# Second round of a two-layer graph kernel: destination spans of 500 in place of 250, with four larger buffers in the ring in place of eight

## The chip, the cores and the metric

The kernel runs on one core of a Trainium2 chip. The metric is the device time of one execution in microseconds; the kernel before has a median of 1175.72 us over 3 runs (1175.63 to 1184.43).

A core has five engines with queues of their own: PE (TensorE, matrix products), DVE (VectorE), ACT (ScalarE), POOL (GpSimd) and SP (SyncE, which here only issues transfers). They meet through semaphores alone. In the rows below PEld is PE's load of the stationary operand of a product.

## The reference

6250 nodes with 96 features, 106250 edges sorted by destination. Two rounds, each followed by a layer norm:

```python
# round 0
h = gelu(x @ W_pre + b_pre)
aggr = segment_sum(h[src] * edge_attr_96, dst)        # messages with edge features
t = x + aggr
x = layernorm(x + (t + gelu(gelu(t @ W1 + b1) @ W2 + b2)))
# round 1
deg = segment_sum(ones, dst); dinv = rsqrt(max(deg, 1))
h = x @ W_lin.T + b_lin
agg = segment_sum(h[src] * (dinv[src] * dinv[dst])[:, None], dst)
out = layernorm(x + relu(agg + x @ W_root.T + b_root))
```

## The kernel before, in words

**Round 0** goes over the edges in 167 units of 5 tiles of 128 edges. For a unit, POOL issues five indirect transfers (line 880) that gather the rows `h[src]` into `gath`, which has room for 8 units; POOL may fill a unit's place when DVE's product of the unit 8 before is done (`s_msg`). SP loads the edge features into `edg`, ACT copies them to `edges_ps` (L1022), DVE compares the destinations with a window's numbers (`onehot`, L1291) and multiplies (`msg`, L1307), and PE sums `msg` against `onehot` into `seg` (L1517). DVE adds a group's window to `sumT`, the sums by node (L1328). As soon as the nodes of a chunk (4 tiles of 128 nodes; the cuts are in `FINE`) are complete, the "step0" phases compute that chunk's new `x`, the table for round 1 as three bf16 summands `parts`, and the root term.

**Round 1** does not gather again. In the first part of the program, beside round 0, a matrix of counts is built: how many edges go from each source node to each destination. DVE builds one-hot rows (`hots_raw`, L1403, L1405), PE multiplies them for pairs of 5 destinations (`count_pair`, L1549; 625 pairs), ACT turns the result into bf16 (`keep_pair`, L970) in one of two `counts` buffers, and SP stores a buffer of 125 destinations to HBM when it is full (`store_counts`, L739; 50 stores of 1531 KB). The sums of round 1 are then dense products: for a span of destinations and a cut of source tiles, SP loads a **piece** of the counts (`load_piece`, L749), and PE multiplies it with the three summands of `parts` for each tile (`sum_piece`, L1571: stationary operand 96 columns of `parts`, moving operand one row of counts as wide as the span). Pieces of one span that stand behind each other form a run in one PSUM bank; DVE adds a finished run to `sumT` or `upper` (`dense`, L1429, and L1423 where an amount kept apart is taken in). While pairs are still counted, only one bank is there for runs, later three. There are 313 pieces in 170 runs.

**Where the pieces stand** is decided by `schedule()` when the program is built: each unit brings a credit of 11 tiles (14 once all pairs are counted), a piece is put in when the credit is at least `CT` = 4, and one piece may follow each pair. A span is ready four units after its last store. All engines follow the one list `order`; SP issues everything in its order, and the load of piece q waits until piece q - `PS` is used (`s_used`), with `PS` buffers in the ring.

At the end the counts for the last cuts of source tiles are multiplied the other way round (`add_counts`, L1652), and the last layer norm runs set by set ("step1").

Of the kernel before, what the change touches and what calls it, by code (L numbers as in the profile page):

```python
# [6 lines left out]
BF16 = mybir.dt.bfloat16  # L7
# [37 lines left out]
CT = 4  # L45
# [33 lines left out]
DN = 2 * GD  # L79
SPANS = N_NODES // DN  # L80
PS = 8

SPLIT = 12
# [16 lines left out]
EAGER_SPANS = SETS[EAGER] // 2  # L100
# [5 lines left out]
assert NT % CT == 1 and len(TAILS) == 1 and SETS[-1] == STORES and STORES % 2 == 0 and STORES * GD == N_NODES  # L106
# [41 lines left out]

def span_end(e):
    return DN * e + DN  # L150

# [11 lines left out]
def schedule():  # L163
# [67 lines left out]
    for u in range(ALL_UNITS):  # L231
# [69 lines left out]
def build(nc, x, xT_in, src, dst, first, tile_first, tile_rows, edge, edge_tail, W_pre, b_pre, W1, b1, W2, b2,  # L301
          WlinT, b_lin, WrootT, b_root, out):
    with ExitStack() as ctx:
# [27 lines left out]
        piece = piece_raw[:].bitcast(BF16).rearrange("p (s h n) -> p s h n", s=PS, h=2)  # L331
# [240 lines left out]
        def is_apart(k):  # L572

            return apart[k // 2] is not None
# [112 lines left out]
        def _(sp):  # L687
# [118 lines left out]
            for item in order:  # L806
# [10 lines left out]
                while loaded < ahead and 2 * pieces[loaded][0] + 2 <= stores_sent:  # L817
# [401 lines left out]
        def _(dve):  # L1219
# [188 lines left out]
            def dense(r):  # L1408

                e, q, is_apart, takes = runs[r]  # L1410
                run_sum = sums(r)[0:D, 0:DN]
                high = upper[:, (e - SPLIT) * DN:(e - SPLIT) * DN + DN] if e >= SPLIT else None
                if is_apart:
                    total = high
                else:
                    total = sumT[0:D, e * DN:e * DN + DN]
# [41 lines left out]
        def _(pe):  # L1458
# [103 lines left out]
            def sum_piece(q):  # L1562
# [5 lines left out]
                for i in range(tiles_in(c)):  # L1568
                    rows = piece[:, q % PS, :, i * GD:(i + 1) * GD]
                    for part in range(3):  # L1570
                        mm = pe.matmul(sums(r)[0:D, 0:DN], parts[:, FINE[c] + i, part, :], rows,  # L1571
# [69 lines left out]
            def add_counts(c, f):  # L1641
# [5 lines left out]
                for t in reversed(range(tiles)):  # L1647
                    if f < CUTS - 1 and (SETS[c] + t) // 2 >= EAGER_SPANS:
                        continue
# [100 lines left out]
```

## Time and profile before

| | |
|---|---|
| median of the runs | 1175.72 us |
| span of the profiled execution | 1626.2 us |
| PE busy / PEld busy | 1089.4 / 924.8 us |
| POOL busy | 813.4 us |
| DVE busy / ACT busy | 744.1 / 585.3 us |
| moved by DMA | 260.26 MB, mean 160 GB/s |
| mean granted clock of PE | 0.811 |

The profiled execution is 450.5 us longer than the median run, so busy shares of its span say little about an execution that isn't profiled. What can be read from it are durations of single instructions, distances between instructions that follow each other with nothing between, and the order in which engines wait for each other.

### The profile page before, as it was taken

To read this page: it belongs to the slowest core of one execution; us is meant where nothing else is said; L and a number is where in the kernel's file an instruction comes from. 1 tells how busy PE (TensorE), PEld (TensorE's weight loads), DVE (VectorE), ACT (ScalarE), POOL (GpSimd) and SP (SyncE) were. 2 spreads that over 40 slices of the span, in tenths; PEclk is the share of its full clock that TensorE was granted. 3 is DMA by queue.
4 is the path that set the end of the run, shared out by engine and by line. 5 is a ranking of instruction groups with operands and counts; after the bars stand their busy time and mean duration, and the time that the engine had idled before them with its cause. 6 is when DMAs were issued, how large, how long until landed. Compare 5 with 4: busy or idle time off the path is not lost. (4 is left out here: it accounts for less than half of the span.)

```text
span 1626.2 us, 21159 instructions
## 1 busy us (share of the span) xinstructions
PE 1089.4 (67%) x7455; PEld 924.8 (57%) x8121; DVE 744.1 (46%) x1460; ACT 585.3 (36%) x1012; POOL 813.4 (50%) x908
## 2 busy tenths in 40 slices
PE   3341465655656766677767777877877876747887
PEld 3341343433444644566657666767777776646787
DVE  6024555546645646455535444532323324233466
ACT  0130355655646556365534445541001011010124
POOL 7355356556555646545534534545555444565202
PEclk9985666777776887878978988988889888878899
DMA  5421165545445547557656556756666655544553
GB/s 151 124 77 29 37 200 169 182 138 187 149 142 182 180 136 230 179 162 239 208 165 200 163 186 212 219 174 189 192 179 187 167 160 147 158 114 128 133 153 77
DMA packets 185721, 260.26 MB, mean 160 GB/s; under 512 B 68650, under 2 KB 163882, under 8 KB 179018
## 3 DMA queue, kind: packets, MB, share of 16 engines
q1 hardware_dynamic: 158328, 215.57, 41.9%
q0 software_dynamic: 26992, 42.82, 11.4%
q8 instruction: 63, 1.03, 0.3%
q10 hardware_dynamic: 290, 0.45, 0.1%
q14 instruction: 48, 0.39, 0.1%
HBM read 173.12 MB, written 85.62 MB: 159 GB/s over the span
## 5 line engine op out<-in xcount | busy, mean ns | idle before, releaser
L880 POOL DMA_INDIRECT gath<-table_h,srcs x791 | 757.2, 957 | 712.2 <-DVE msg L1307 491.4
L1571 PE MATMUL bank_q<-piece_raw,early_late 128*96 128x250 bf16 x3453 | 460.2, 286 | 74.4 <-issue 55.6
L1571 PEld LDWEIGHTS bank_q<-piece_raw,early_late 128*96 128x96 bf16 x3453 | 403.0, 131 | 76.8 <-issue 72.8
L1517 PE MATMUL seg<-onehot,msg 128*97 128x128 f32 (+1 forms) x1662 | 297.5, 341 | 136.9 <-DVE sumT L1328 63.7
L970 ACT CAST counts_raw<-bank_q 128x490 bf16<-128x490 f32 x400 | 281.1, 747 | 268.7 <-PE bank_q L1549 117.6
L1307 DVE TENSOR_TENSOR msg<-gath,edges_ps 128x480 f32<-128x480 f32 x166 | 107.8, 650 | 411.3 <-ACT edges_ps L1022 351.0
L1517 PEld LDWEIGHTS seg<-onehot,msg 128*97 128x97 f32 x1662 | 258.0, 215 | 60.6 <-DVE msg L1307 32.9
L1549 PE MATMUL bank_q<-hots_raw 128*128 128x245 bf16 x834 | 183.5, 319 | 141.5 <-ACT counts_raw L970 101.1
L970 ACT CAST counts_raw<-bank_b 128x490 bf16<-128x490 f32 x200 | 149.8, 749 | 144.0 <-remote 49.8
L1022 ACT COPY edges_ps<-edg 128x480 f32<-128x480 f32 x166 | 98.8, 595 | 262.7 <-DVE msg L1307 227.2
L1405 DVE TENSOR_TENSOR hots_raw<-counters,kb 128x1960 bf16<-128x1960 bf16 (+1 forms) x157 | 182.6, 1163 | 0.0
L1549 PEld LDWEIGHTS bank_q<-hots_raw 128*128 128x128 bf16 x834 | 72.4, 107 | 192.9 <-ACT counts_raw L970 137.3
L1464 PEld LDWEIGHTS <-w_pre 97*128 97x128 bf16 x666 | 69.4, 112 | 162.4 <-DVE sumT L1328 66.7
L1549 PE MATMUL bank_b<-hots_raw 128*128 128x245 bf16 x416 | 95.8, 318 | 88.2 <-ACT counts_raw L970 53.9
L1429 DVE TENSOR_TENSOR sumT<-sumT,bank_q 96x250 f32<-96x250 f32 x126 | 51.7, 411 | 190.5 <-remote 114.1
L1291 DVE TENSOR_TENSOR onehot<-counters,rel 128x640 f32<-128x640 f32 (+1 forms) x166 | 131.6, 793 | 0.0
L1403 DVE TENSOR_TENSOR hots_raw<-counters,kb 128x1024 bf16<-128x1024 bf16 (+1 forms) x157 | 106.8, 680 | 52.8 <-remote 35.5
L1549 PEld LDWEIGHTS bank_b<-hots_raw 128*128 128x128 bf16 x416 | 35.6, 107 | 115.0 <-ACT counts_raw L970 72.1
L1328 DVE TENSOR_TENSOR sumT<-sumT,seg 97x128 f32 (+1 forms) x62 | 17.1, 275 | 73.8 <-remote 59.7
L1429 DVE TENSOR_TENSOR upper<-upper,bank_q 96x250 f32<-96x250 f32 x31 | 12.7, 410 | 73.5 <-remote 50.5
L859 POOL DMA_INDIRECT gath<-in_x,srcs x40 | 38.5, 963 | 12.9 <-issue 11.9
L892 POOL TENSOR_TENSOR gap<-bns 125x5 f32<-125x5 f32 x9 | 1.8, 201 | 74.2 <-DVE bns L1189 74.2
(212 smaller groups left out, 655.6 us busy)
## 6 DMA issues: line engine op xcount, KB each, us to landing
counts_hbm<-counts_raw SPq DMA_DIRECT2D x50, 1531.2 KB
piece_raw<-counts_hbm SPq DMA_DIRECT2D x250, 250.0 KB
edg<-in_edge SPq DMA_DIRECT2D x166, 240.0 KB
gath<-table_h,srcs POOLq DMA_INDIRECT x791
piece_raw<-counts_hbm SPq DMA_DIRECT2D x38, 125.0 KB
piece_raw<-counts_hbm SPq DMA_DIRECT2D x25, 187.5 KB
counts_raw<-counts_hbm SPq DMA_DIRECT2D x4, 625.0 KB
table_h<-stage SPq DMA_DIRECT2D x12, 192.0 KB
```

The lines of the kernel that those rows point to most:

```text
L880: pool.indirect_dma_start(gath[0:k, u % GS * UT + j, :], None, table[0], bass.IndirectOffsetOnAxis(ap=srcs[0:k, t:t + 1], axis=0)).then_in ...
L970: act.copy(counts[:, k % 2, :, i * WD:(i + 2) * WD].rearrange("p a (w n) -> p w a n", w=2), counted).then_inc(s_kept, 1)
L1022: act.copy(edges_ps[:, 0:UT * D], edg[:, u % ES].rearrange("p j d -> p (j d)")).then_inc(s_eps, 1)
L1291: dve.tensor_tensor(onehot[:, s, :, 0:w], iota_ps[:, 0:w].unsqueeze(1).to_broadcast([P, UT, w]), rel[:, u * UT:(u + 1) * UT].unsqueeze(2). ...
L1307: dve.tensor_tensor(msg[:, s, :, 0:D], gath[:, slot_tiles(u), :], by_tile(edges_ps, UT), ALU.mult).then_inc(s_msg, 1)
L1403: dve.tensor_tensor(hot_b(j)[:, 0:n], iota_b.unsqueeze(1).to_broadcast([P, n, P, 2]), blocks.unsqueeze(2).to_broadcast([P, n, P, 2]), ALU. ...
L1405: dve.tensor_tensor(hot_k(j)[:, 0:n], iota_k.unsqueeze(1).to_broadcast([P, n, KC, 2]), keys.unsqueeze(2).to_broadcast([P, n, KC, 2]), ALU. ...
L1429: dve.tensor_tensor(total, total, run_sum, ALU.add).then_inc(s_dense, 1)
L1464: pe.ldweights(w_pre[:].bitcast(BF16)[:, 0:P])
L1517: last = pe.matmul(seg[0:D + 1, half(g)], msg[0:k, u % MS, j, :], onehot[0:k, u % MS, j, 0:reach(g)], start=(u == first_unit(g) and j == 0 ...
L1549: last = pe.matmul(pair_bank(m)[:, w * KC:(w + 1) * KC], hot_b(j)[:, i, :, w], hot_k(j)[:, i, :, w], start=True, stop=True)
L1571: mm = pe.matmul(sums(r)[0:D, 0:DN], parts[:, FINE[c] + i, part, :], rows, start=(first and i == 0 and part == 0), stop=(last and i == til ...
```

## The change

A span is now four stores wide: 500 destinations, in 13 spans, of which the last has two stores (250). A piece of four tiles has 500 KB, and the ring has four of them in place of eight of 250 KB, the same memory. The schedule counts a piece of a full span with twice its tiles, and asks for a credit of 8.

```diff
-DN = 2 * GD
-SPANS = N_NODES // DN
-PS = 8
-SPLIT = 12
+HALVES = 4
+DN = HALVES * GD
+SPANS = -(-STORES // HALVES)
+PS = 4
+SPLIT = 6
...
+def span_sets(e):
+    return range(HALVES * e, min(HALVES * e + HALVES, STORES))
...
+def span_nodes(e):
+    return slice(DN * e, span_end(e))
+def cost_of(e, c):
+    return tiles_of_cut(c) * len(span_sets(e)) // 2
...
-            if ready and stored[2 * e + 1] + 4 <= u:
-                gain = FINE[upto(e)] - FINE[summed[e]]
+            if ready and stored[span_sets(e)[-1]] + 4 <= u:
+                gain = (FINE[upto(e)] - FINE[summed[e]]) * len(span_sets(e)) // 2
...
-            if credit >= CT:
+            if credit >= 2 * CT:
...
-                    credit -= tiles_of_cut(pieces[-1][1])
+                    credit -= cost_of(*pieces[-1][0:2])
                 else:
-                    credit = min(credit, 2.0 * CT)
+                    credit = min(credit, 4.0 * CT)
...
-                    sp.wait_ge(s_store[s], 16 * (e + 1))
+                    sp.wait_ge(s_store[s], 16 * len(range(s, span_sets(e).stop, 2)))
...
-                sp.dma_start(piece[:, q % PS, :, 0:tiles_in(c) * GD],
-                             counts_hbm[2 * e:2 * e + 2, :, cols].rearrange("h b n -> b h n")
+                sp.dma_start(piece[:, q % PS, 0:len(sets), 0:tiles_in(c) * GD],
+                             counts_hbm[sets.start:sets.stop, :, cols].rearrange("h b n -> b h n")
...
-                        mm = pe.matmul(sums(r)[0:D, 0:DN], parts[:, FINE[c] + i, part, :], rows,
+                        mm = pe.matmul(sums(r)[0:D, 0:len(span_sets(e)) * GD], parts[:, FINE[c] + i, part, :], rows,
```

The list that results has 163 pieces in 92 runs. Of its 1797 products 1656 are 500 wide and 141 are 250 wide; before there were 3453, all 250 wide. The columns are the same: 2 x 1656 + 141 = 3453 widths of 250. Destinations whose sum is kept apart for a while (`upper`) are the same ones, as are the products of the end.

On PE, in a unit of the stage in which pairs are still counted (before, unit 100). `hots_raw` products are pairs, `piece_raw` products are pieces, `seg` is round 0's unit:

```order
L1517 MATMUL seg<-onehot,msg 97x128 x5
L1464 LDWEIGHTS w_pre
L1549 MATMUL bank_b<-hots_raw 128x245 x2
L1464 LDWEIGHTS w_pre
L1571 MATMUL bank_q2<-piece_raw,early_late 96x250 x9
L1549 MATMUL bank_q0<-hots_raw 128x245 x2
L1571 MATMUL bank_q2<-piece_raw,early_late 96x250 x12
L1549 MATMUL bank_q1<-hots_raw 128x245 x2
L1571 MATMUL bank_q2<-piece_raw,early_late 96x250 x12
L1549 MATMUL bank_b<-hots_raw 128x245 x2
L1571 MATMUL bank_q2<-piece_raw,early_late 96x250 x12
```

The same place after the change:

```order
L1532 MATMUL seg<-onehot,msg 97x128 x5
L1479 LDWEIGHTS w_pre
L1564 MATMUL bank_b<-hots_raw 128x245 x2
L1586 MATMUL bank_q2<-piece_raw,early_late 96x500 x12
L1564 MATMUL bank_q0<-hots_raw 128x245 x2
L1586 MATMUL bank_q2<-piece_raw,early_late 96x500 x12
L1564 MATMUL bank_q1<-hots_raw 128x245 x2
L1564 MATMUL bank_b<-hots_raw 128x245 x2
L1479 LDWEIGHTS w_pre
L1564 MATMUL bank_q0<-hots_raw 128x245 x2
L1564 MATMUL bank_q1<-hots_raw 128x245 x2
```

Between two pairs there now stand twelve products of 500 columns where twelve of 250 stood, and fewer places hold a piece.

On PE behind the last pair (before, units 127 and 128), three runs are touched in two units:

```order
L1517 MATMUL seg<-onehot,msg 97x128 x5
L1571 MATMUL bank_q1<-piece_raw,early_late 96x250 x12
L1464 LDWEIGHTS w_pre
L1571 MATMUL bank_q2<-piece_raw,early_late 96x250 x24
L1464 LDWEIGHTS w_pre
L1571 MATMUL bank_q0<-piece_raw,early_late 96x250 x12
L1464 LDWEIGHTS w_pre
L1517 MATMUL seg<-onehot,msg 97x128 x5
L1571 MATMUL bank_q0<-piece_raw,early_late 96x250 x12
```

After the change, the same units:

```order
L1532 MATMUL seg<-onehot,msg 97x128 x5
L1479 LDWEIGHTS w_pre
L1586 MATMUL bank_q0<-piece_raw,early_late 96x500 x24
L1479 LDWEIGHTS w_pre
L1532 MATMUL seg<-onehot,msg 97x128 x5
L1479 LDWEIGHTS w_pre
L1586 MATMUL bank_q1<-piece_raw,early_late 96x500 x12
```

Here a unit holds one or two pieces where it held three or four, and each `LDWEIGHTS w_pre` ahead of a run, which waits for the bank, is there half as often.

## Rows read from the trace of the kernel before

**Rows 1.** The page's costliest groups: busy us, mean ns | idle before, releaser

```profile
L880 POOL DMA_INDIRECT gath<-table_h,srcs x791 | 757.2, 957 | 712.2 <-DVE msg L1307 491.4
L1571 PE MATMUL bank_q<-piece_raw,early_late 128*96 128x250 bf16 x3453 | 460.2, 286 | 74.4 <-issue 55.6
```

**Rows 2.** POOL in order of time, its first gathers: start, us, [idle before <-releaser]

```profile
94.82 0.95 POOL L880 DMA_INDIRECT gath<-table_h,srcs  x1 [35.05 <-DVE msg L1307]
96.07 0.95 POOL L880 DMA_INDIRECT gath<-table_h,srcs  x1 [0.30 <-issue]
...
137.36 0.94 POOL L880 DMA_INDIRECT gath<-table_h,srcs  x1 [0.30 <-issue]
146.22 5.63 POOL L880 DMA_INDIRECT gath<-table_h,srcs  x1 [7.92 <-DVE msg L1307]
...
178.46 0.94 POOL L880 DMA_INDIRECT gath<-table_h,srcs  x1 [20.62 <-DVE msg L1307]
```

**Rows 3.** POOL in order of time, its last gather

```profile
1528.07 1.11 POOL L880 DMA_INDIRECT gath<-table_h,srcs  x1 [9.95 <-DVE msg L1307]
```

**Rows 4.** The chain that ended last: the last unit, the first and last products of the end

```profile
1577.40 0.14 DVE onehot L1298
...
1580.12 0.23 DVE sumT L1328
1580.35 0.12 issue
1580.47 1.45 PE bank_q L1632 x10
...
1612.14 1.74 PE bank_q L1652 x30
```

**Rows 5.** Timeline at 1300 us: pieces on PE in a stretch at full pace, and one where they stop

```profile
1300.09 2.56 PEld L1571 LDWEIGHTS bank_q<-piece_raw,early_late 128*96 128x96 bf16 x24
1303.95 0.52 PE L1571 MATMUL bank_q<-piece_raw,early_late 128*96 128x250 bf16 x3 [0.43 <-issue]
1305.38 0.59 PE L1571 MATMUL bank_q<-piece_raw,early_late 128*96 128x250 bf16 x4 [0.91 <-issue]
1307.50 0.78 PE L1571 MATMUL bank_q<-piece_raw,early_late 128*96 128x250 bf16 x4 [1.53 <-issue]
...
1317.92 1.12 PEld L1517 LDWEIGHTS seg<-onehot,msg 128*97 128x97 f32 x10
1319.10 5.60 PE L1571 MATMUL bank_q<-piece_raw,early_late 128*96 128x250 bf16 x48
...
1322.73 0.64 DVE L1307 TENSOR_TENSOR msg<-gath,edges_ps 128x480 f32<-128x480 f32 x1
1325.17 0.68 DVE L1108 TENSOR_TENSOR colsT<-sumT,xTc 97x512 f32<-97x512 f32 x1
1326.50 0.64 DVE L1307 TENSOR_TENSOR msg<-gath,edges_ps 128x480 f32<-128x480 f32 x1
```

**Rows 6.** Timeline at 949 us: pieces between pairs

```profile
949.27 0.20 PEld L1549 LDWEIGHTS bank_q<-hots_raw 128*128 128x128 bf16 x2
949.49 1.31 PEld L1571 LDWEIGHTS bank_q<-piece_raw,early_late 128*96 128x96 bf16 x12
950.47 0.61 ACT L1022 COPY edges_ps<-edg 128x480 f32<-128x480 f32 x1
950.78 0.20 PEld L1549 LDWEIGHTS bank_q<-hots_raw 128*128 128x128 bf16 x2
951.00 1.31 PEld L1571 LDWEIGHTS bank_q<-piece_raw,early_late 128*96 128x96 bf16 x12
951.12 0.66 DVE L1307 TENSOR_TENSOR msg<-gath,edges_ps 128x480 f32<-128x480 f32 x1 [0.62 <-issue]
```

**Rows 7.** Line views of L970 and L1429: duration ns min/median/max

```profile
L970 ACT CAST counts_raw<-bank_q x400: 697/736/853, 184.1 to 1094.0; 128x490 bf16<-128x490 f32 x134
L1429 DVE TENSOR_TENSOR sumT<-sumT,bank_q x126: 404/411/415, 554.0 to 1578.7; 96x250 f32<-96x250 f32 x126
```

**Rows 8.** Transfers by line: KB each, us from issue to landing

```profile
edg<-counts_hbm SPq DMA_DIRECT2D x1, 312.5 KB, 5.4
edg<-counts_hbm SPq DMA_DIRECT2D x1, 187.5 KB, 5.0
```

**Rows 9.** Stretches: us, PE (x) PEld (x) DVE (x) ACT (x) POOL (x), PEclk, DMA share, GB/s

```profile
700.00:800.00 100.00, 78.23 (x519) 65.05 (x560) 57.95 (x97) 56.35 (x96) 56.52 (x60) 0.83 0.67 212
1100.00:1200.00 100.00, 81.56 (x599) 73.07 (x625) 28.52 (x66) 9.21 (x17) 54.35 (x58) 0.87 0.65 190
```

More of the change, by code:

```diff
@@ L99 @@
 EAGER = 5
-EAGER_SPANS = SETS[EAGER] // 2
+EAGER_SPANS = SETS[EAGER] // HALVES
 LOADED = (0, 1, 2, 3, 7, 4, 5, 6)
@@ L105 @@
 assert REM > 0 and UT * D <= 512 and EARLY <= GS and NW * WD == N_NODES
-assert NT % CT == 1 and len(TAILS) == 1 and SETS[-1] == STORES and STORES % 2 == 0 and STORES * GD == N_NODES
+assert NT % CT == 1 and len(TAILS) == 1 and SETS[-1] == STORES and STORES * GD == N_NODES
 assert CUTS - 1 == next(c for c in range(CUTS) if FINE[c] == NT - 2) and FINE[CUTS - 2] == NT - 4
@@ L146, in last_pair_of @@
     return (k * GW + GW - 1) // 2
+def span_sets(e):
+    return range(HALVES * e, min(HALVES * e + HALVES, STORES))
 def span_end(e):
-    return DN * e + DN
+    return GD * span_sets(e).stop
+def span_nodes(e):
+    return slice(DN * e, span_end(e))
+def cost_of(e, c):
+    return tiles_of_cut(c) * len(span_sets(e)) // 2
 def span_chunk(e):
@@ L330, in build @@
         piece_raw = sb("piece_raw", [P, PS * CT * DN // 2])
-        piece = piece_raw[:].bitcast(BF16).rearrange("p (s h n) -> p s h n", s=PS, h=2)
+        piece = piece_raw[:].bitcast(BF16).rearrange("p (s h n) -> p s h n", s=PS, h=HALVES)
         hots_raw = sb("hots_raw", [P, 2 * BP * (P + KC)])
@@ L572, in is_apart @@
         def is_apart(k):
-            return apart[k // 2] is not None
+            return apart[k // HALVES] is not None
         def tiles_in(c, cuts=FINE):
@@ L748, in load_piece @@
                 cols = slice(FINE[c] * GD, FINE[c + 1] * GD)
-                sp.dma_start(piece[:, q % PS, :, 0:tiles_in(c) * GD],
-                             counts_hbm[2 * e:2 * e + 2, :, cols].rearrange("h b n -> b h n")
+                sets = span_sets(e)
+                sp.dma_start(piece[:, q % PS, 0:len(sets), 0:tiles_in(c) * GD],
+                             counts_hbm[sets.start:sets.stop, :, cols].rearrange("h b n -> b h n")
                              ).then_inc(s_piece[q % PS], 16)
@@ L816, in _ @@
                     ahead = min(item[1] + PS, len(pieces))
-                while loaded < ahead and 2 * pieces[loaded][0] + 2 <= stores_sent:
+                while loaded < ahead and span_sets(pieces[loaded][0]).stop <= stores_sent:
                     load_piece(loaded)
@@ L1410, in dense @@
                 e, q, is_apart, takes = runs[r]
-                run_sum = sums(r)[0:D, 0:DN]
-                high = upper[:, (e - SPLIT) * DN:(e - SPLIT) * DN + DN] if e >= SPLIT else None
+                nodes = span_nodes(e)
+                run_sum = sums(r)[0:D, 0:nodes.stop - nodes.start]
+                high = upper[:, nodes.start - SPLIT * DN:nodes.stop - SPLIT * DN] if e >= SPLIT else None
                 if is_apart:
@@ L1415, in dense @@
                 else:
-                    total = sumT[0:D, e * DN:e * DN + DN]
+                    total = sumT[0:D, nodes]
                     dve.wait_ge(s_base, span_chunk(e) + 1)
@@ L1568, in sum_piece @@
                 for i in range(tiles_in(c)):
-                    rows = piece[:, q % PS, :, i * GD:(i + 1) * GD]
+                    rows = piece[:, q % PS, 0:len(span_sets(e)), i * GD:(i + 1) * GD]
                     for part in range(3):
-                        mm = pe.matmul(sums(r)[0:D, 0:DN], parts[:, FINE[c] + i, part, :], rows,
+                        mm = pe.matmul(sums(r)[0:D, 0:len(span_sets(e)) * GD], parts[:, FINE[c] + i, part, :], rows,
                                        start=(first and i == 0 and part == 0),
@@ L1647, in add_counts @@
                 for t in reversed(range(tiles)):
-                    if f < CUTS - 1 and (SETS[c] + t) // 2 >= EAGER_SPANS:
+                    if f < CUTS - 1 and (SETS[c] + t) // HALVES >= EAGER_SPANS:
                         continue
```

## The prediction

> **What bounds the kernel now.** I read the page's costliest groups first, because the profiled span (1626.2 us) is 450.5 us longer than the median run, and busy shares of such a span mislead. The largest group is POOL's gathers: 791 of them, 0.957 us each, and most of their idle time is a wait for DVE's product [rows 1]. So either POOL sets the pace, or whoever frees its buffers does.
>
> Next POOL in order of time. Gathers that wait for nothing follow each other at a strict distance: from 94.82 to 137.36 us there are 35, so 42.54 / 34 = 1.251 us each, 0.95 busy and 0.30 between [rows 2]. Five make 6.26 us a unit. Then POOL has filled its 8 places and waits for DVE, which is held up by the preparation of the count tables; the gathers run on from 178.46 us [rows 2]. By then 40 of 791 are issued, and 751 are left. If POOL never waited again it would need 751 x 1.251 = 939.5 us, up to 1118.0. In the profile the last gather starts at 1528.07, and waits for DVE even there [rows 3]: POOL had been a full 8 units ahead, and the others set the pace of the profiled execution.
>
> From the last unit's work (1577.40) to the end of the span there are 48.8 us of chain, all of it DVE and PE one behind the other [rows 4]. Put behind a POOL that never waits: 1118.0 + 1.1 for the last gather + about 3 for its landing and the product (my estimate: half of the 5.0 us of the smaller transfer in [rows 8], and 0.6 for the product) + 48.8 = 1171 us. The median is 1175.72. In other terms: of the profile's excess, 1349.6 - 939.5 = 410 us are POOL's waits and 46 us the eight units still open at the end, together 456 of the 450.5 by which the two executions differ. **The execution that is timed looks like one in which the gathers set the pace from 178 us on**, with some 5 us left for everything else. I can't see it directly; it rests on a head and a pace that I take over unchanged from the profile.
>
> Can the others keep 6.26 us a unit? PE makes 24 weight loads of pieces in 2.56 us, 0.107 us a product, and 48 products in 5.60 us [rows 5]. At the stage of units 80 to 109 the list holds 972 products, 32.4 a unit: 3.5 us. Add 1.1 to 1.2 for the unit's own ten loads [rows 5], 6.15 pairs at 0.22 (1.4 us) [rows 6], and some 0.2 for waits and the chunk's steps: 6.2 to 6.4 us. In units 110 to 139, with 1230 products, it is 4.4 + 1.2 + 0.3 = 5.9. So PE is about as loaded as POOL and has eight units of room to be late in, 50 us. Singly, units do reach such paces in the profile: two products of DVE stand 3.77 us apart at 1322.73 and 1326.50 [rows 5]. But pieces also stop with nothing to wait for, three or four products and then 0.4 to 1.5 us of "issue" [rows 5]; I take these stops as belonging to the profiled execution, since the median has no room for them.
>
> **The change, part by part.**
>
> *Wider products.* 250 columns take 0.107 us, of which 250 / 2.4 GHz = 0.104 are columns; the granted clock is 0.83 to 0.87 in the mean of these stages [rows 9], and these rows are at its upper level. So weight loads are already hidden and only 0.003 us a product is left to win. 500 columns: 0.208 + 0.003 = 0.211 at best, 2 x 0.107 = 0.214 at worst. PE's sum goes from 3453 x 0.107 = 369.5 to 1656 x 0.211 + 141 x 0.107 = 364.5 us: 5 us less, bounds 0 and 5. That the weight side is not the limit shows at the other end too: the 96-column products of the end take 1.74 / 30 = 0.058 us [rows 4], far below 0.107, so loading is quick enough for 250 columns.
>
> The Trainium skill, "TensorE: Matmul & The Clock Gate", Back-to-back issue gap, gives a stream of load and product pairs as about 131 ns each at 512 columns and 81 ns at 128. By that the 1656 wide products would take 217 us and PE would gain some 137; the row at 250 columns (0.107) is what its columns alone take and doesn't lie on a line between those two, so I don't count on it.
>
> *Runs.* 92 in place of 170: 78 waiting weight loads fewer, 0.04 us each, 3 us of PE. DVE adds 92 sums in place of 170. At 250 columns one takes 0.411 us [rows 7]; a 512-column sum from SBUF takes 0.68 [rows 5], which I take for 500. 170 x 0.411 = 69.9 becomes 92 x 0.68 = 62.6: 7 us less on an engine that is under 60% busy [rows 9]. Worth nothing while POOL sets the pace.
>
> *Transfers.* The same bytes in 163 issues in place of 313. SP's issues are not on the path. A piece of 500 KB lands later: 187.5 KB take 5.0 us and 312.5 KB 5.4 [rows 8], so 0.4 per 125 KB, and 500 KB about 6.0. When PE begins piece q, piece q + 3 may be loaded; three pieces of 12 x 0.211 make 7.6 us of cover, and behind the last pair, where a unit has two pieces, there are the units' own products besides. Before it was 7 x 1.28 = 9.0 us of cover for about 5.2. The cover shrinks from 3.8 to 1.6 us and still holds; if it failed by 1 us a piece in the 56 pieces of units 110 to 139, that is 56 us, little more than the eight units of room.
>
> *The order.* Between two pairs there are now 2.53 us of piece in place of 1.28. ACT copies the next unit's edge features behind the second pair, so the way from one unit's product on PE to the next unit's is: 1.2 (unit) + 0.22 + 2.53 + 0.22 + 0.74 (ACT's pair) + 0.61 + 0.66 (DVE's product) [rows 5 to 7] = 6.2 us, with handovers 6.4. Before it was 1.25 less, 5.1. Units with two or three pieces (11 of the 32 units 80 to 111) take PE 1.2 + 1.4 + 2 x 2.53 + 0.2 = 7.9 us. Mean: (21 x 6.4 + 11 x 7.9) / 32 = 6.9, that is 0.65 over POOL's pace and 21 us over the stage. This lateness fits into the 50 us of room, and behind unit 112 PE needs 5.9 us a unit and catches up 0.36 x 35 = 13 us by unit 146; units 147 to 150 hold no piece and give the rest back.
>
> Sum on the path that sets the end: 0 from PE and DVE, 0 from the transfers, 0 from the order while the room lasts, 0 from the end, which is the same. 1175.72 + 0 = **1175 us**.
>
> **The rivals.**
>
> *POOL doesn't set the pace, its users do* (faster). If the head is shorter in the timed execution than in the profile, the 5 us left over grow, and PE, at 6.2 to 6.4 us a unit in units 80 to 109, is the bound there. Then PE's 8 us (5 + 3) count, and the 48 products that leave this stage (972 become 924 widths) move 5 us into units with room: 1175 - 13 = 1162 us. For it: PE is the busiest engine of the profile in both stages [rows 9]. Against it: the sum of the gathers hits the median within 5 us. Chance 0.20 for a gain over 1%.
>
> *A wide product is cheaper than its columns* (faster still), as the page has it: on a POOL-bound kernel it gives nothing, on a PE-bound one down to the gathers' 1171 less what the head hides, so about 1160. Chance 0.03, within the 0.20.
>
> *Thicker pieces starve ACT and DVE while pairs are counted* (slower). The mechanism is the 2.53 us between two pairs, as above. It decides when the consumers enter unit 80 with less than 21 us of room, that is when the first stage has not let them catch up with POOL. Then all of it shows: 1175 + 21 = 1196 us; with half of the room gone, 1187. For it: POOL starts this stage a full eight units ahead at 178.46 us [rows 2], so the consumers start with no room at all. Against it: the stage to unit 80 has no or few pieces. Chance 0.17. *A ring of four that runs dry* behind unit 112 would cost up to 56 us, less what the room takes: 1180 to 1200. Chance 0.05.
>
> *The change does nothing*: that is my forecast, chance 0.58.
>
> **How the numbers follow.** About 1% is what a measurement of this kernel can tell from no change, so the borders are 1164 and 1187. Likeliest 1175 (0.58, own range 1168 to 1182). Faster 0.20, slower 0.22. For 8 in 10 the range takes the gain of PE with the moved products and a little more (1160), and the full price of the thicker pieces (1198).
>
> **What would show it.** In the changed kernel's profile: 500-wide products at 0.211 to 0.214 us in unbroken stretches (0.13 would be the page's rule); gathers still 1.25 us apart where they don't wait; DVE's sums at about 0.68 us. The profiled span may well fall by tens of us, since PE's stops come between its instructions and there are 1656 products and 1734 weight loads fewer; that would say nothing of the median. Thicker pieces show as longer waits of ACT's L970 and of DVE's product for `edges_ps` between 600 and 1100 us, a dry ring as PE idle ahead of L1586 with a landing as its end. Wrong would be the forecast if the timed execution were not paced by the gathers, above all if their 0.30 us gaps were shorter without the profiler.

## The result, and the profile after

The changed kernel takes **1217.84 us** (median of 4 runs, 1214.60 to 1221.01), against 1177.18 for the kernel before in the runs it is compared with. The ratio is 1.035 with a 95% interval of 1.030 to 1.040: about 41 us slower. The prediction said 1175 us, no change.

The profiled execution of before whose rows stand above was a disturbed one (its span of 1626.2 us is far from any timed run), so the kernel before was profiled again; from here on "before" is this second profile, with a span of 1180.4 us, and the 32.4 us between it and the profile of after (1212.8 us) are what has to be explained. (The medians differ by 41 us; the second profile is an execution from the slower end of before's runs, that of after its fastest.)

The pages' costliest groups, busy us and mean ns, then idle before and its main releaser. Before, second profile, where [rows 1] had 460.2 us of products and 712.2 us of idle POOL:

```profile
L880 POOL DMA_INDIRECT gath<-table_h,srcs x791 | 760.2, 961 | 284.8 <-issue 231.3
L1571 PE MATMUL bank_q<-piece_raw,early_late 128*96 128x250 bf16 x3453 | 409.1, 273 | 9.1 <-DVE early_late L1163 3.7
```

After:

```profile
L894 POOL DMA_INDIRECT gath<-table_h,srcs x791 | 758.6, 959 | 308.9 <-issue 228.0
L1586 PE MATMUL bank_q<-piece_raw,early_late 128*96 128x500 bf16 (+1 forms) x1797 | 400.6, 375 | 6.5 <-DMA piece_raw<-counts_hbm 3.5
L1444 DVE TENSOR_TENSOR sumT<-sumT,bank_q 96x500 f32<-96x500 f32 x65 | 43.6, 670 | 95.5 <-PE bank_q L1586 94.8
```

The stops inside pieces of [rows 5] are gone from both: they belonged to the disturbed execution, as supposed. PE's pieces wait for nothing worth naming. So the loss isn't in the time of the products, and hardly in the ring: PE waits 3.5 us for landings.

**Where the time went.** The borders of the windows are the products (`msg`) of units 80, 110, 150 and the last one, then the end; columns as in [rows 9]. Before:

```profile
571.00:797.00 226.00, 199.88 (x1679) 180.36 (x1793) 145.48 (x240) 145.64 (x237) 143.82 (x152) 0.98 0.83 261
797.00:1030.00 233.00, 227.49 (x2049) 222.67 (x2192) 113.20 (x265) 42.12 (x71) 173.49 (x183) 1.00 0.89 261
1030.00:1132.00 102.00, 88.63 (x734) 84.75 (x830) 62.29 (x183) 20.28 (x36) 56.74 (x60) 0.92 0.68 178
1132.00:1180.00 48.00, 37.66 (x529) 37.00 (x573) 29.04 (x139) 22.30 (x65) 11.55 (x63) 0.92 0.36 88
```

After, the same four stretches:

```profile
570.00:821.00 251.00, 207.90 (x1176) 136.74 (x1283) 146.76 (x234) 141.49 (x236) 142.18 (x151) 0.94 0.74 233
821.00:1051.00 230.00, 226.83 (x1346) 159.71 (x1450) 106.99 (x223) 41.75 (x70) 172.16 (x181) 1.00 0.87 263
1051.00:1161.00 110.00, 92.06 (x491) 63.25 (x558) 58.88 (x154) 20.28 (x36) 57.91 (x61) 0.88 0.63 169
1161.00:1213.00 52.00, 41.07 (x516) 40.30 (x561) 27.65 (x135) 22.30 (x65) 11.56 (x63) 0.86 0.32 78
```

Unit 80 starts 1.5 us earlier than before. Then come 25 us of loss in units 80 to 109 (8.36 us a unit where it was 7.53), 3 us of gain in units 110 to 149, 8 us of loss from unit 150 to the last product (unit 166), and 4 in the end. In the first stretch PE is idle for 43 us in place of 26, and no other engine is fuller: nobody is busy, everybody waits. For whom, the waits say (us in total, times, longest). Before:

```profile
DVE msg L1307 <- ACT edges_ps L1022: 213.0, 76, 31.6
ACT counts_raw L970 <- PE bank_q L1549: 133.7, 115, 5.2
POOL gath L880 <- DVE msg L1307: 53.4, 32, 5.5
```

After:

```profile
DVE msg L1321 <- ACT edges_ps L1036: 247.0, 81, 31.6
ACT counts_raw L984 <- PE bank_q L1564: 160.1, 92, 4.5
POOL gath L894 <- DVE msg L1321: 80.9, 43, 5.5
```

All three waits grow by 26 to 34 us, and they are links of one chain: DVE's product waits for ACT's copy of the edge features, ACT for PE's pair, POOL for DVE. The timeline of one turn in after shows the links (start, us, engine, line; in brackets idle time and who ended it):

```profile
760.90 0.65 DVE L1321 TENSOR_TENSOR msg<-gath,edges_ps 128x480 f32<-128x480 f32 x1 [3.87 <-ACT edges_ps L1036]
...
761.47 0.66 DVE L1444 TENSOR_TENSOR sumT<-sumT,bank_q 96x500 f32<-96x500 f32 x1
...
762.06 0.68 DVE L1417 TENSOR_TENSOR hots_raw<-counters,kb 128x1024 bf16<-128x1024 bf16 x1
762.66 1.17 DVE L1419 TENSOR_TENSOR hots_raw<-counters,kb 128x1960 bf16<-128x1960 bf16 x1
...
763.92 0.40 PE L1564 MATMUL bank_q<-hots_raw 128*128 128x245 bf16 x2 [0.54 <-DVE hots_raw L1419]
...
764.16 2.07 PE L1586 MATMUL bank_q<-piece_raw,early_late 128*96 128x500 bf16 x9
...
766.07 0.38 PE L1564 MATMUL bank_b<-hots_raw 128*128 128x245 bf16 x2
...
766.49 0.73 ACT L984 CAST counts_raw<-bank_b 128x490 bf16<-128x490 f32 x1 [1.40 <-PE bank_b L1564]
...
767.07 0.61 ACT L1036 COPY edges_ps<-edg 128x480 f32<-128x480 f32 x1
767.71 0.65 DVE L1321 TENSOR_TENSOR msg<-gath,edges_ps 128x480 f32<-128x480 f32 x1 [1.47 <-ACT edges_ps L1036]
```

**The loop.** DVE's product, the sum of a finished run, `hots_raw` in two steps, first pair, a whole piece, second pair, ACT's cast of it, ACT's copy into `edges_ps`, DVE's next product. From start to start: 0.57 + 0.59 + 0.60 + 1.26 + 0.24 + 1.91 + 0.42 + 0.58 + 0.64 = 6.81 us. The piece here has nine products; with twelve it is 0.64 more, 7.4 us. With a piece of 1.28 us in place of 2.53, as in before, the same sum gives 6.2 (worked out, not read from a turn of before). Measured are 8.36 and 7.53 us a unit; the 0.9 to 1.3 us between are not split further. Candidates are steps of the chunks that lie in some units' way (DVE's and PE's of L1159 and L1491, for example) and, in after, pieces that run at the lower clock (its mean is 0.94 in this stretch, that of before 0.98). Of all links ACT's copy is the odd one: it needs nothing of the pairs and stands behind the second of them only because `schedule()` puts it at place 2 of each unit.

### The profile page after: what moved, and what is told of

It reads as the page before. It is cut to its first block and busy times, and to the rows that moved or that the text cites. A ratio compares the mean times of both kernels' runs of the same rounds, so it can differ in the third digit from the quotient of the medians.

```text
span 1212.8 us, 17246 instructions
## 1 busy us (share of the span) xinstructions
PE 979.9 (81%) x5799; PEld 699.8 (58%) x6387; DVE 732.7 (60%) x1376; ACT 578.2 (48%) x1012; POOL 814.6 (67%) x908
## 5 line engine op out<-in xcount | busy, mean ns | idle before, releaser
L1586 PE MATMUL bank_q<-piece_raw,early_late 128*96 128x500 bf16 (+1 forms) x1797 | 400.6, 375 | 6.5 <-DMA piece_raw<-counts_hbm 3.5
L1532 PE MATMUL seg<-onehot,msg 128*97 128x128 f32 (+1 forms) x1662 | 252.8, 308 | 81.8 <-DVE msg L1321 46.4
L1586 PEld LDWEIGHTS bank_q<-piece_raw,early_late 128*96 128x96 bf16 x1797 | 218.6, 125 | 139.3 <-issue 13.2
L1532 PEld LDWEIGHTS seg<-onehot,msg 128*97 128x97 f32 x1662 | 223.3, 190 | 47.6 <-DVE msg L1321 46.0
L1564 PE MATMUL bank_q<-hots_raw 128*128 128x245 bf16 x834 | 168.2, 299 | 62.1 <-ACT counts_raw L984 50.4
L1564 PEld LDWEIGHTS bank_q<-hots_raw 128*128 128x128 bf16 x834 | 68.8, 104 | 121.1 <-ACT counts_raw L984 97.3
L1564 PE MATMUL bank_b<-hots_raw 128*128 128x245 bf16 x416 | 89.6, 300 | 29.4 <-ACT counts_raw L984 24.6
L1479 PEld LDWEIGHTS <-w_pre 97*128 97x128 bf16 x588 | 58.0, 107 | 95.2 <-DVE sumT L1342 34.0
L1444 DVE TENSOR_TENSOR sumT<-sumT,bank_q 96x500 f32<-96x500 f32 x65 | 43.6, 670 | 95.5 <-PE bank_q L1586 94.8
L996 ACT ACTIVATE y<-bank_a,b1c 96x512 f32<-96x512 f32 (+2 forms) x14 | 8.8, 630 | 38.5 <-PE bank_a L1601 38.5
```

Source lines behind the costliest of these rows:

```text
L1444: dve.tensor_tensor(total, total, run_sum, ALU.add).then_inc(s_dense, 1)
L1479: pe.ldweights(w_pre[:].bitcast(BF16)[:, 0:P])
L1532: last = pe.matmul(seg[0:D + 1, half(g)], msg[0:k, u % MS, j, :], onehot[0:k, u % MS, j, 0:reach(g)], start=(u == first_unit(g) and j == 0 ...
L1564: last = pe.matmul(pair_bank(m)[:, w * KC:(w + 1) * KC], hot_b(j)[:, i, :, w], hot_k(j)[:, i, :, w], start=True, stop=True)
L1586: mm = pe.matmul(sums(r)[0:D, 0:len(span_sets(e)) * GD], parts[:, FINE[c] + i, part, :], rows, start=(first and i == 0 and part == 0), sto ...
```

## The experiments

**0. Before once more**, unchanged, for the second profile.

> The kernel before, unchanged, for a second profile, since the first one's span is 450 us over its median. All theories: a time of 1174 to 1185 us and, if the first profile was disturbed, a span close to that. Theory A (thick pieces between two pairs starve ACT): units 80 to 110 take 6.3 to 7.3 us each here against 8.2 to 8.7 in the changed kernel, and ACT waits for PE's pairs less there. Theory B (the ring of four): the same units, but the difference is PE's idle time ahead of its pieces. Theory C (wide spans become ready later, with one bank for runs): the difference is waits for a run's bank and for DVE's sums.

Measured: 1182.22 us in that one execution, span 1180.4; its rows are those of before shown above.

The theory: **the loop through ACT's copy paces units 80 to 109; its length grows with the PE time of a piece between two pairs, whatever the width of a product.** Rivals: the wide products or spans themselves cost the time; the ring of four is too small for 500 KB; the two stages only trade a fixed amount of PE work. Pieces can be made thick and thin at either width, so the two can be told apart. "Pace" below is the time from the product of unit 80 to that of unit 110, divided by 30, from each run's profile.

**1. After, pieces in halves between pairs.** A piece of four tiles is loaded as before, but PE does two of its tiles at one place and the other two at the next, with a pair between:

```diff
-            if credit >= 2 * CT:
+            if owed:
+                rest()
+            elif credit >= 2 * CT:
...
-                for i in range(tiles_in(c)):
+                half = (tiles_in(c) + 1) // 2
...
+                for i in (range(half) if part_of_it == 0 else range(half, tiles_in(c))):
```

> The changed kernel, but a piece is multiplied in two halves of at most two tiles with one pair between them while pairs are counted; spans, ring, transfers, widths and runs are those of the changed kernel. Theory A (2.5 us of piece between two pairs leave ACT without work, and the next unit's edge copy late): 1175 to 1192 us. Theories B (ring of four) and C (spans of 500 and their runs): 1205 to 1225 us, as the changed kernel.

Measured: 1180.78 us, ratio to before 1.001 (0.998 to 1.005). Pace 7.34 us, below the 7.53 of before. Wide products, the ring of four and 500 KB are all still in, and the loss is gone. That already speaks against width and ring as its cause in this stage: units 80 to 109 take 220 us in place of 251. Units 150 to the end still take 159 us, against 162 in after and 150 in before.

**2. Before, made thick.** Two 250-wide pieces of one place, with a credit of 8, so 2.56 us of PE between two pairs:

```diff
-            if credit >= CT:
+            if credit >= 2 * CT:
...
+                    if len(pieces) > was and (open_run or u > built + 1):
+                        next_piece(u, next(n for until, n in LEAST if u < until))
...
-                    credit -= tiles_of_cut(pieces[-1][1])
+                    credit -= sum(tiles_of_cut(x[1]) for x in pieces[was:])
```

> The kernel before with its spans of 250 and its ring of eight, but the schedule waits for a credit of 8 and then puts two pieces behind each other at one place, so that 2.57 us of piece stand between two pairs as in the changed kernel. Theory A: 1198 to 1220 us. Theories B, C and D (the 500-wide product itself, its clock or its DVE sum): 1172 to 1183 us, as the kernel before.

Measured: 1210.01 us, ratio 1.025 (1.020 to 1.030), pace 8.3 us. The loss appears without any wide product: of the 33 us between the profiles, 24 lie in units 80 to 109, as in after. It is experiment 1 the other way round. Units 150 to 166 are slower too, 111.6 us where before took 101.6; see "The late loss".

**3. Before with a ring of four.** `PS = 4` in place of 8, still 250 KB each, memory layout unchanged.

> The kernel before with a ring of four buffers of 250 KB in place of eight, half the memory ahead that both kernels have. Theory A: 1174 to 1186 us. Theory B (too little ahead): at least 20 us slower, 1196 to 1230 us.

Measured: 1221.43 us, ratio 1.040 (1.032 to 1.048), pace 7.8 us. Here PE does wait for the loads:

```profile
L1571 PE MATMUL bank_q<-piece_raw,early_late 128*96 128x250 bf16 x3453 | 415.2, 274 | 38.5 <-DMA piece_raw<-counts_hbm 29.9
```

So a ring can cost as much as the whole result, and a view that the ring doesn't matter on this kernel is wrong. But these are four pieces of half the size: 3 x 1.28 = 3.8 us of cover against the 5.0 to 5.4 of [rows 8]. In after the same wait is 3.5 us (page row above), since its cover is 3 x 2.53 us.

**4. After in halves, ring of three.** Experiment 1's order (in its general form, as in experiment 5) with `PS = 3`.

> The changed kernel with split pieces (1180.78 with a ring of four) and a ring of three buffers of 500 KB. Theory B in its weak form (the ring of four is at its edge): 1195 to 1230 us, with waits of PE for landings. If four buffers of 500 KB have cover to spare, as forecast (7.6 us against 6.0): 1179 to 1190 us.

Measured: 1196.81 us, ratio 1.015 (1.009 to 1.020), 16 us behind experiment 1; PE's wait for landings is now 14.4 us in 10 places. With two pieces of cover (2 x 2.53 = 5.1 us) the ring is too small. That three are enough isn't shown by this run, whose time lies in the range expected for a ring of four at its edge, but by after itself, where PE waits 3.5 us for landings in all. The prediction's sum on the ring holds.

**5. The same halves everywhere.** In experiment 1 pieces are whole again once all pairs are counted. Here they stay in halves to the end.

```diff
-            if not pairs:
-                rest()
```

> The changed kernel with pieces in halves through the whole program: behind the last pair too the second half stands one place later, so that the steps of a chunk in the last units come between halves (1.27 us) and not whole pieces (2.53 us). The split while pairs are counted alone gave 1180.78, with a last stage from unit 150 of 111 us against 102 in the kernel before. If the thick pieces among the steps cause that: 1165 to 1176 us. If it is the sum of work in the last units: 1177 to 1185 us.

Measured: 1181.72 us, ratio 1.003 (0.999 to 1.007): the same as experiment 1. Nothing is to be had from halves where no pairs are counted. The late loss isn't removed by halving the pieces: units 150 to the end take 162 us, as in after.

**6 to 9. The dose.** Thinner still: after in single tiles (0.64 us) while pairs are counted, then everywhere; and before in halves, which is also 0.64 us. `PART` is the number of tiles done at one place:

```diff
+PART = 1
...
-                for i in range(tiles_in(c)):
+                for i in range(k * PART, min(k * PART + PART, tiles_in(c))):
```

> The changed kernel with pieces in single tiles (0.63 us each, 500 wide) between pairs while pairs are counted, whole behind them. The same thickness as in the split kernel before, with wide products. Theory A with the dose from 2.53 us (1217.84) over 1.27 us (1180.78): 1160 to 1176 us. If 500-wide spans cost something of their own while pairs are counted (readiness, one bank), it stays 5 us or more above the split kernel before.

> The changed kernel with pieces in single tiles of 0.63 us everywhere, one at a place, so that they also stand between the steps of the last units. With single tiles while pairs are counted only it gave 1170.77; its units 150 to 166 and the end took 109 + 52 us where the split kernel before took 99 + 48, with one wait of PE of 3.75 us and a lower clock behind it. If few thick pieces leave nothing to put between the steps of the last units: 1156 to 1166 us, and the 3.75 us wait is gone. If it is something else of the wide spans: 1168 to 1175 us.

> The kernel before (spans of 250, ring of eight) with its pieces in halves of at most two tiles, 0.64 us of piece between two pairs in place of 1.28. Theory A (time of piece between two pairs, against 0.74 us of ACT a pair): ACT is never without a pair, units 80 to 110 fall from 7.5 us towards 7.0, so 1160 to 1172 us. If thickness matters only beyond 1.3 us, or if something else limits ACT: 1174 to 1182 us, as the kernel before.

Measured: 1170.77 us (0.993, 0.990 to 0.996), 1167.93 us (0.991, 0.987 to 0.996), and for before in halves 1154.76 us (0.978, 0.971 to 0.985), below the 1160 to 1172 expected for it. **And before in single tiles** (0.32 us between pairs):

> The kernel before with single tiles of 250 columns (0.32 us) between pairs. Dose of theory A: 1.28 us gave 1178, 0.64 us gave 1154.76. ACT needs 0.74 us a pair, PE 0.22; with 0.32 us of piece a pair PE is ahead of ACT and blocked by the three banks until the parts owed run out. No more gain is expected: 1150 to 1160 us, and over 1160 if single tiles run out of places between the pairs.

Measured: 1140.98 us, ratio 0.970 (0.961 to 0.979), below the 1150 to 1160 expected. The paces, each from one profile, make one table:

| between two pairs | with 500 wide | with 250 wide |
|---|---|---|
| 2.5 us | 8.36 (after) | 8.3 (experiment 2) |
| 1.3 us | 7.34 (experiment 1) | 7.53 (before) |
| 0.64 us | 6.97 (single tiles) | 6.9 (halves) |
| 0.32 us | | 6.45 (single tiles, with less work) |

The last row can't be read as a dose. A narrow piece in four single tiles takes four places, and the list then has room for fewer pieces: in units 80 to 109 PE makes 738 products of 250 columns where before in halves makes 918, which alone is 180 x 0.107 = 19 us, 0.6 us a unit and so more than the 0.45 between the paces. The pieces moved into later units (629 behind unit 150 in place of 517). In the other runs of the table the stage holds 900 to 984 widths of 250.

In the rows above it, the columns agree within 0.2 us at each thickness, and from 2.5 to 0.64 us of PE between pairs the pace falls by 1.4 us for 1.9. The pace goes by thickness, not by width. The totals don't agree as well: at 0.64 us, after is 16 us behind before (18.5 in the profiles), of which these 30 units hold only 2. 7 us lie ahead of unit 80, 4 are won back in units 110 to 149, and 14 lie behind unit 150. See "The late loss".

**10. After with the copy first.** The link itself: ACT's copy for the next unit stands ahead of the unit's first pair in place of behind the second. Nothing else changes; pieces are whole and wide.

```diff
-            if i == 2 and 0 < u < UNITS:
+            if i == 0 and 0 < u < UNITS:
                 order.append(("edges", u + 1))
```

> The changed kernel with whole thick pieces; only the place of ACT's copy of the next unit's edge features moves ahead of the unit's first pair, from behind the second. It tells apart two ways in which thick pieces hurt. If the loss is that the copy, and with it DVE's product and the gathers' buffers, wait behind a pair that stands behind 2.53 us of piece: 1185 to 1200 us. If it is that ACT has no pair to turn in those 2.53 us and so can't turn all pairs of a unit in time: 1210 to 1222 us.

Measured: 1144.09 us, ratio 0.973 (0.964 to 0.981), and so 74 us less than after by one number in the list, far below the 1185 to 1200 us expected even if the copy's place was the cause. DVE's and POOL's waits of before and after shrink or vanish; the page's row and two waits:

```profile
L894 POOL DMA_INDIRECT gath<-table_h,srcs x791 | 762.4, 964 | 243.0 <-issue 238.4
```

```profile
DVE msg L1321 <- ACT edges_ps L1036: 75.1, 32, 31.5
ACT counts_raw L984 <- PE bank_q L1564: 109.5, 69, 3.8
```

POOL's idle time is 243.0 us, of which 238.4 are the 0.30 us steps between gathers: it hardly waits for anyone any more. And the timeline shows the copy and the product beside the piece, not behind it:

```profile
704.23 0.62 ACT L1036 COPY edges_ps<-edg 128x480 f32<-128x480 f32 x1
...
705.04 2.07 PE L1586 MATMUL bank_q<-piece_raw,early_late 128*96 128x500 bf16 x9
...
705.24 0.73 ACT L984 CAST counts_raw<-bank_q 128x490 bf16<-128x490 f32 x1 [0.40 <-PE bank_q L1564]
...
706.96 0.38 PE L1564 MATMUL bank_b<-hots_raw 128*128 128x245 bf16 x2
707.05 0.64 DVE L1321 TENSOR_TENSOR msg<-gath,edges_ps 128x480 f32<-128x480 f32 x1
```

Where the gain lies says why it is larger than the loss that was looked for. Of the 71 us between the profiles of after and of this run, 38 lie in units 80 to 109 and 32.5 ahead of unit 80, a stretch in which after loses nothing against before: units 50 to 79 take 6.43 us each here, 6.96 in before and 7.08 in after. So the copy's place costs time in both kernels and over a longer stretch; thick pieces only lengthen its loop further from unit 80 on.

ACT's cast of the pairs still waits 109.5 us for PE. So the form of the theory in which thick pieces starve ACT, the words of the prediction's slower rival, falls for the most part: ACT still waits that long in a kernel that is 74 us faster, because the copy doesn't stand behind the wait.

**11 and 12. The same edit in before, and its opposite.**

> The kernel before with the edge copy ahead of the first pair, nothing else. Theory L (the loop through DVE's tables, the first pair, a piece, the second pair and the edge copy paces units 50 to 110 in both kernels): 1125 to 1145 us. If wide spans cost something of their own, this stays below the changed kernel with the copy first (1144.09) by 5 us or more; if they don't, the two are equal within 5 us. If the loop paces only the changed kernel: 1170 to 1180 us.

> The kernel before with the edge copy one place later, behind the third pair: its loop gets another piece of 1.28 us, a pair of 0.22 and 0.74 us of ACT in units that hold three pieces or more, and 0.74 to 1 us in the others. Theory L: 1 to 2 us a unit in units 80 to 110 and some in 50 to 80, so 1205 to 1240 us. If the loop does not pace the kernel before: 1174 to 1182 us.

```diff
-            if i == 2 and 0 < u < UNITS:
+            if i == 3 and 0 < u < UNITS:
```

Copy first in before: 1135.04 us, ratio 0.965 (0.958 to 0.972). Copy behind the third pair, so that two pieces of 1.28 us lie in the loop: 1218.77 us, ratio 1.035 (1.026 to 1.045), pace 8.1 us. The same units, about 80 to 110, in the first and in the second:

```profile
536.00:745.00 209.00, 191.36 (x1656) 174.13 (x1770) 144.72 (x240) 143.09 (x235) 158.41 (x167) 1.00 0.88 281
```

```profile
594.00:837.00 243.00, 204.81 (x1694) 185.90 (x1810) 144.95 (x240) 146.47 (x237) 142.10 (x151) 0.96 0.78 246
```

Units 80 to 109 take 209 us in the first and 243 in the second, against 226 in before. So the loop through the copy is lengthened and shortened by the copy's place alone, in an otherwise unchanged kernel. That the second ends at the time of after (1217.84 us) is a coincidence of totals: it loses 23 us ahead of unit 80 and 17 in units 80 to 109 (0.56 us a unit, less than the 1 to 2 expected) and nothing behind them, where after loses nothing ahead of unit 80, 25 in that stage and 12 behind unit 150.

Experiments 10 and 11 together give what the thick, wide pieces cost in units 80 to 109 without the loop: 212.9 us against 208.9. Of the 25 us of loss in this stage, 21 are gone when the copy goes first. With experiments 1 and 2, I take the loop as shown for this stage.

**13 to 15. Both edits together.**

> The kernel before with pieces in halves (1154.76) and the edge copy ahead of the first pair. If the copy's place costs something at this thickness: 1140 to 1152 us. If ACT's pairs alone limit: 1152 to 1158 us.

> The changed kernel with the edge copy first and its pieces in single tiles of 0.63 us everywhere, so that they also fill places between the steps of the last units. Against the changed kernel with the copy first alone (1144.09): if thick and few pieces among the last steps cost what the traces suggest (8 to 10 us and a lower clock), 1130 to 1140 us; else 1141 to 1147 us.

> The kernel before with single tiles between pairs and the edge copy first. With halves and the copy first it gave 1126.28, with single tiles alone 1140.98. The gathers alone give about 62 + 791 x 1.25 + 52 = 1103 us. 1115 to 1128 us.

Before in halves with the copy first: **1126.28 us, ratio 0.957 (0.948 to 0.965)**, the fastest kernel here, 4.3% under the one before. Before in single tiles with the copy first: 1131.49 us (0.962, 0.954 to 0.969). After in single tiles with the copy first: 1133.27 us (0.965, 0.957 to 0.973). All three are within 7 us. The first beat the 1140 to 1152 us expected, the second missed its 1115 to 1128. In the last one the chain of the page leads back to the gathers; its shares of the span by engine:

```profile
POOL 41%; PE 25%; issue 14%; DVE 6%; DMA 4%; ACT 3%; DVEq 0%; SPq 0%; ACTq 0%
```

The last gather starts at 1063 to 1064 us in each kernel with the copy first, whatever its width, and at 1103.83 in before and 1126.30 in after:

```profile
1064.29 0.90 POOL L894 DMA_INDIRECT gath<-table_h,srcs  x1 [0.30 <-issue]
```

(this is experiment 10's). From the first gather at 61.9 that is 1002.4 / 790 = 1.269 us each. POOL waits for nobody there; most steps are 1.25 us, and a few longer ones, up to 5.5 us, raise the mean. These kernels have reached the gathers' pace.

**The late loss.** 12 us of the 32 lie behind unit 150, and they stay when the loop is cut: with the copy first and whole pieces, after is 9 us slower than before (1144.09 against 1135.04). In the last units PE of after has a gap that before has not, and runs slowly behind it:

```profile
1141.58 1.90 PE L1532 MATMUL seg<-onehot,msg 128*97 128x64 f32 x10 [3.75 <-DVE sumT L1342]
```

The same unit in before:

```profile
1114.27 0.85 PE L1571 MATMUL bank_q<-piece_raw,early_late 128*96 128x250 bf16 x6 [1.79 <-DVE sumT L1429]
1115.52 1.07 PE L1517 MATMUL seg<-onehot,msg 128*97 128x64 f32 x10 [0.40 <-DVE sumT L1328]
```

Ten products of a unit take 1.90 us in place of 1.07. The granted clock (behind the five engines) in after from 1141 and in before from 1114:

```profile
1141.00:1147.00 6.00, 4.50 (x18) 3.56 (x20) 3.41 (x11) 0.94 (x2) 0.00 (x0) 0.50 0.39 101
```

```profile
1114.00:1119.00 5.00, 3.22 (x25) 2.67 (x30) 3.56 (x11) 1.01 (x3) 0.00 (x0) 1.00 0.56 143
```

0.50 is the 1.2 GHz level, 1.00 the one of 2.4 GHz. Neither the width of a product nor the ring of four is needed for this. The trace of experiment 2, with 250-wide spans, eight buffers and a credit of 8, has the same gap and the same clock behind it, and its units 150 to 166 take 111.6 us, where after takes 109.6 and before 101.6:

```profile
1141.94 1.87 PE L1519 MATMUL seg<-onehot,msg 128*97 128x64 f32 x10 [3.74 <-DVE sumT L1330]
```

```profile
1142.00:1148.00 6.00, 4.57 (x18) 3.42 (x19) 3.43 (x12) 0.68 (x2) 0.00 (x0) 0.50 0.32 80
```

What experiment 2 shares with after, and before does not, is that the list asks for a credit of 8 and puts eight tiles' worth of piece in at one time, half as often. The gap of 3.74 or 3.75 us is there too in experiments 1, 4, 5, 6 and 10, which keep that credit; with single tiles everywhere (7 and 14) it is 3.1 us. So the late loss in units 150 to 166 goes with the coarser list, not with wide spans; the likely way, that PE has no piece left to lay between the short phases of the last chunks, is argued and no run tests it. Thin pieces hardly touch it: units 150 to the end take 163 us in experiment 7 and 158 in 14, against 162 in after. Of the 12.7 us between the profiles of experiments 10 and 14, 13 lie ahead of unit 110 (with 2 lost and 2 won behind it), so the range that 14 hit was hit for another reason than the one expected.

The 4 us of the end are a matter of the clock. In the first 8 to 10 us behind the last unit's product the granted clock is 0.66 in after and 0.57 in experiment 2, and their ends take 52.0 and 52.7 us; it is 1.00 in before and in experiments 1 and 10, and the ends take 48.5, 48.0 and 48.1. But it is also 0.72 in experiment 13, which is narrow, and the end takes 53.2 us. So these 4 us don't belong to the width either, and not for certain to the change.

## Why the prediction was wrong, point by point

**What bounds the kernel: wrong, by a coincidence.** The prediction took the head from a disturbed profile: a first gather at 94.82 and free running from 178.46 us [rows 2]. In the undisturbed profile of before the first one comes at 61.99:

```profile
61.99 0.94 POOL L880 DMA_INDIRECT gath<-table_h,srcs  x1 [2.28 <-DVE msg L1307]
```

The distance of 1.251 us was right for most steps. With the true head the gathers alone give 62.0 + 790 x 1.251 = 1050.3 for the last one, and 1103 with the 52.9 us that the sum put behind it, not 1171. The last gather of before in fact starts at 1103.8 and 76.6 us follow it. So 53.5 + 23.7 = 77 us that the sum lacked stood against a head that was 68 us too long (1118.0 against 1050.3), and the sum met the median within 5 us by luck. Experiment 11, in which POOL waits for nobody, splits the 77: its last gather starts at 1063.6 and 69.2 us follow. 13 us are the few longer steps between gathers, 40 are POOL's waits for the loop, 16 are missing behind the last gather even without the loop, since the last product comes 21 us after it and not 4, and 7 are the loop's there. The prediction said itself that head and pace weren't seen in a timed execution; it should have asked for more than one total to agree.

**"The order": the right mechanism, and this step of it mis-sized.** "The way from one unit's product on PE to the next unit's is: ... = 6.2 us, with handovers 6.4. Before it was 1.25 less, 5.1." The way closes not on PE's unit product but on DVE's tables: behind its product DVE still has a run's sum (0.67) and `hots_raw` (0.68 + 1.17) to do before the next unit's first pair can start. These 2.45 us (0.59 + 0.60 + 1.26 in the timeline) were left out and PE's 1.2 us, which lie beside them, put in. So the 6.2 should have read 7.4 and the 5.0 without handovers 6.2, and with the steps that hang in the loop they measure 8.36 and 7.53. At 5.1 the loop lay below POOL's 6.26 and was no bound of before; measured at 7.53 it was the bound already, and experiment 11 shows it by taking 42 us from before with the copy's place alone.

**"0 from the order while the room lasts", "This lateness fits into the 50 us of room": wrong, and this is the step that cost the forecast.** The lateness was put at 21 us, and the stage gave 25. That is near, but in part by luck: it was 0.65 us a unit over POOL's 6.26, where the runs have 0.83 over the loop's own 7.53. The room was not there. POOL's lead in before is used up by unit 90: DVE's product starts 43 to 44 us behind the end of its unit's last gather at unit 80 in both kernels, 52 (before) and 61 (after) at unit 90, and 53 and 62 at unit 110, where the eight places are full. With the copy first it is 9 us at unit 80 in both. The prediction named the condition, "when the consumers enter unit 80 with less than 21 us of room", and gave it 0.17. With the loop at its right length it would have seen that the room is eaten before unit 80.

**Wide products: right.** 23 in a row take 5.06 us in after, with 0.37 for the last one (5.06 - 0.37) / 22 = 0.213 us each; predicted were 0.211 to 0.214.

```profile
875.21 5.06 PE L1586 MATMUL bank_q<-piece_raw,early_late 128*96 128x500 bf16 x23
```

The Trainium skill, "TensorE: Matmul & The Clock Gate", Back-to-back issue gap, gives 131 ns for a stream of load and product pairs at 512 columns, and about N / 2.4 + 2.5 ns for a single one. The measured stream follows the second form (an estimate of 211 ns at 500 by that page), not the first.

**Runs and DVE's sums: the price right.** 0.670 us each against 0.68 predicted. "Worth nothing" isn't shown: such a sum stands in the loop, though the columns of the table differ by 0.2 us at most. **The ring: right**, experiments 3 and 4 bracket it. **PE's gain where it is bound**: units 110 to 149 gave 3 us.

**The end: "0 from the end, which is the same": the products are the same, and the profiles of after and before differ by 4 us there,** with the clock as said above. The 8 us of units 150 to 166 are a cost of the coarser list for which the prediction has no term.

The range ended at 1198 with the whole price of the rival. It would have needed the rival's price, the late loss, and a median of before that isn't tied to the gathers.

## What to carry to other kernels

A loop between engines has to be followed until it returns to the instruction it began with, with everything that each engine does in order in between, for both kernels; if the loop of before then comes out below its measured pace, a link is missing. Where work is put between two small steps that others wait for, its longest undivided piece counts: here, changing the size from 2.5 us to 1.3 was worth 37 us, and moving one 0.6 us copy of another engine ahead of the wait 74 us. A total alone doesn't tell causes apart: two kernels that end at 1218 and 1219 us lost their time in different stages. And a sum that meets a measured total proves little when its inputs come from an execution 450 us longer: profile again before building on it.

## What the runs showed of the hardware that was not expected

- A profiled execution can be disturbed as a whole: two profiles of one unchanged kernel had spans of 1626.2 and 1180.4 us, first gathers at 94.82 and 61.99 us, and 460.2 and 409.1 us for the same 3453 products. The distances of instructions that wait for nothing (1.25 us for gathers, 0.107 to 0.108 us for products) were the same in both.
- A gap of 3.75 us on PE was followed by a stretch at the 1.2 GHz level in which a unit's ten products took 1.90 us in place of 1.07. The same gap was followed by a granted clock of 0.50 in experiment 2 (from 1142 to 1148 us) and in experiment 10 (from 1075 to 1085 us). In the first two the products of the same unit took 1.90 and 1.87 us, so there the gap cost more than its length.
